# First head of each attention group turned by VectorE and through DRAM instead of by TensorE

## What is computed

```python
q = (x @ wq)            # 16 heads of 128
k, v = x @ wk, x @ wv   # 4 heads of 128, each shared by 4 query heads
# causal attention with a running softmax over chunks of 128 keys
x = layernorm(x + attention(q, k, v) @ wo)
logits = clip(xt @ gate_w.T, -50, 50)     # 8 experts, the two best per token
rw = softmax(top 2)
weighted = (softmax(expert_atom_weights) @ atoms) * sigmoid(importance)
# sparse expert rows: contrib[t, row] += x[t, col] * sum_k rw[t, k] * weighted[expert_k]
x = layernorm(x + xt @ W.T + contrib)
```

## Time and profile before

| | us |
|---|---|
| median of 3 runs | 1833.12 |
| profiled execution | 1836.27 |
| its span | 1834.5 |
| TensorE busy | 1774.3 (97%) |
| VectorE busy | 1238.0 (67%) |
| ScalarE busy | 823.1 (45%) |
| GpSimd busy | 799.0 (44%) |

### The profile page before, as it was taken

One profiled execution on the slowest core, in us unless ns is written; L12 is line 12 of the kernel. 1 busy time (PEld: TensorE's weight loads), 2 busy tenths in 40 slices (PEclk: granted clock), 3 DMA queues, 4 the chain that ended last, 5 costly groups with the idle time before them and its releaser, 6 DMA issues.

```text
span 1834.5 us, 33331 instructions
## 1 busy us (share of the span) xinstructions
PE 1774.3 (97%) x9290; PEld 1502.0 (82%) x9290; DVE 1238.0 (67%) x3881; ACT 823.1 (45%) x2058; POOL 799.0 (44%) x1093
## 2 busy tenths in 40 slices
PE   8999999999999999999999999999999999999982
PEld 7888888888888888888888888888888888778872
DVE  5566467776777577757775777677776777763355
ACT  4444344434444444544454444454444443434454
POOL 6775345544554333323332333233323334666564
PEclk9999999999999999999999999999999999999996
DMA  9665443335333455454444445454445338545788
GB/s 329 223 226 195 164 141 116 116 110 168 116 116 110 150 162 153 150 174 149 154 150 159 134 152 160 154 177 158 150 133 198 135 107 314 173 161 166 251 314 318
DMA packets 156287, 315.83 MB, mean 172 GB/s; under 512 B 23008, under 2 KB 66176, under 8 KB 145600
## 3 DMA queue, kind: packets, MB, share of 16 engines
q1 hardware_dynamic: 137808, 273.74, 44.2%
q0 software_dynamic: 18288, 39.80, 7.1%
HBM read 226.25 MB, written 87.23 MB: 171 GB/s over the span
## 4 chain that ended last, share of the span: by engine, by line
PE 85%; DVE 4%; issue 3%; POOL 2%; DMA 2%; ACT 1%; DVEq 0%; POOLq 0%; ACTq 0%; SPq 0%
PE psum L1541 23%; PE psum L1543 23%; PE psum L1542 23%; PE psum L1568 7%; PE psum L2298 2%; PE psum L2299 2%; PE psum L2300 2%; PE psum L372 1%; DMA token_rows<-x,ids_now 1%; ACT probs L1818 1%; PE psum L788 1%; DVE pT_lo L1942 1%; POOL expert_weights L1435 1%; POOL probs L1415 0%; DMA chosen_rows<-y_rows,slot_now 0%
## 5 line engine op out<-in xcount | busy, mean ns | idle before, releaser
L1415 POOL TENSOR_SCALAR probs<-probs,row_inv 128x128 f32<-128x128 f32 (+3 forms) x512 | 308.0, 625 | 435.1 <-DVE row_inv L1939 433.2
L1818 ACT ACTIVATE probs<-probs,neg_max 128x512 f32<-128x512 f32 (+3 forms) x512 | 282.4, 554 | 361.4 <-DVE neg_max L1931 359.4
L1541 PE MATMUL psum<-xT_hi,w_hi 128*128 128x512 f32 x640 | 252.5, 394 | 0.7 <-DVE qT_lo L1956 0.7
L1931 DVE CUSTOM_DVE_ANT_0 probs<-psum,causal 128x512 f32<-128x512 f32 (+3 forms) x512 | 223.4, 487 | 42.7 <-issue 20.4
L1543 PE MATMUL psum<-xT_hi,w_lo 128*128 128x512 f32 x640 | 250.2, 391 | 0.0
L1542 PE MATMUL psum<-xT_lo,w_hi 128*128 128x512 f32 x640 | 249.9, 390 | 0.0
L1942 DVE TENSOR_TENSOR pT_lo<-psum,pT_hi 128x512 fp32r<-128x512 f32 (+1 forms) x384 | 206.5, 593 | 19.7 <-ACT pT_hi L1828 19.5
L1828 ACT CAST pT_hi<-psum 128x512 fp32r<-128x512 f32 (+1 forms) x384 | 172.3, 526 | 65.2 <-PE psum L1568 65.2
L1541 PE MATMUL psum<-wo_hi,oT_hi 128*128 128x512 f32 x496 | 196.8, 397 | 0.0
L1543 PE MATMUL psum<-wo_hi,oT_lo 128*128 128x512 f32 x496 | 194.0, 391 | 0.0
L1542 PE MATMUL psum<-wo_lo,oT_hi 128*128 128x512 f32 x496 | 193.6, 390 | 0.0
(11 more groups left out here) (250 smaller groups left out, 3870.4 us busy)
## 6 DMA issues: line engine op xcount, KB each, us to landing
w_hi<-split_qk_weights SPq DMA_DIRECT2D x140, 256.0 KB, 2.7
w_lo<-split_qk_weights SPq DMA_DIRECT2D x140, 256.0 KB, 3.0
wo_hi<-split_out_weights SPq DMA_DIRECT2D x27, 1024.0 KB, 5.5
wo_lo<-split_out_weights SPq DMA_DIRECT2D x27, 1024.0 KB, 7.6
expert_weights_hi_lo<-split_expert_weights SPq DMA_DIRECT2D x8, 2048.0 KB, 10.0
x_in<-in_L_attn_x_dram SPq DMA_DIRECT2D x8, 1024.0 KB, 7.3
expert_weights<-fill SPq DMA_DIRECT2D x16, 512.0 KB, 4.4
piece_raw<-expert_weights SPq DMA_DIRECT2D x16, 512.0 KB, 5.9
```

The costliest lines, as they stand in the source:

```text
L1415: last = pool.tensor_scalar(p, p, row_inv[:, buf, i:i + 1], 1.0, ALU.mult, ALU.mult)
L1541: pe.matmul(dst, hi_s, hi_m, start=start, stop=False)
L1818: last = act.activation(probs[:, buf, a:a + w], probs[:, buf, a:a + w], ACT.Exp, bias=neg_max[:, buf, i:i + 1], scale=-1.0, accum_out=row_ ...
L1931: last = dve.tensor_tensor_reduce(probs[:, buf, a:a + w], psum[:, BANK_S + bank, col:col + w], causal[:, T - w:T], -1.0, -MASKED, ALU.add, ...
```

## The change

In batches 1 to 7, but not in the last iteration (`is_moved`), the first head of a group is not turned on TensorE. VectorE turns it in squares of 32 x 32 inside each 32 partitions (`turn_blocks`, 5 instructions, 1280 columns), SyncE stores the result to DRAM (`strips`) and reads it back with four transfers that put the squares at their partitions (`move`), and one copy of ScalarE and one subtraction of VectorE make the halves of all 1280 columns (`moved_pT`). Query 2 is projected right after scores(n + 1), and scores(n + 2) come ahead of the second filler. The fourth head is turned between query 0 and query 1 of the next iteration. In "group" iterations that are moved, the key is now projected ahead of values 0/1 and query 0 goes to the key's bank, as in "first" (`is_key_first`, `banks_as`). The buffers of the expert pieces become single ones to make room. On GpSimd `route_rstd` stands behind a `normalize` instead of ahead of it.

```diff
+SQUARE = 32
+SIDE = P // SQUARE
+MOVED_FROM = HKV
+MOVES = 16 * (1 + SIDE)
...
+        self.blocks = arena("probs_blocks", [P, SIDE, PACK // SIDE])
+        self.moved = moved("probs_moved", [P, SIDE, PACK // SIDE])
+        self.piece_raw = piece_raw("piece_raw", [P, PIECE * NE])
...
+def is_moved(kind, route):
+    return route and kind != "end"
+
+def is_key_first(kind, route):
+    return kind == "first" or is_moved(kind, route) and kind == "group"
+
+def lows_done(n, k, kind, route):
+    if is_moved(kind, route):
+        return 3 * (n + (0, 0, 1, 3)[k]) + 3
+    return 3 * (n + k) + 3
...
SyncE
+        def move(it, k, free):
+            wait_apart(sp, s_blocks, moved_number(it, k) + 1, s_passed)
+            sp.dma_start(strips[k], F.blocks[:].rearrange("p j f -> p (j f)")).then_inc(s_moved, 16)
+            wait_apart(sp, s_pt_lo, free, s_passed)
+            wait_apart(sp, s_moved, 32 + MOVES * moved_number(it, k), s_passed)
+            for j in range(SIDE):
+                src = strips[k, :, j * PACK // SIDE:(j + 1) * PACK // SIDE].rearrange("(i p) f -> p i f", p=SQUARE)
+                sp.dma_start(F.moved[j * SQUARE:(j + 1) * SQUARE], src).then_inc(s_moved, 16)
+
         def iteration(b, g, it, kind, route, job):
+            n = it * G
             after, second = (g + 1) % HKV, (g + 2) % HKV
+            if is_moved(kind, route):
+                move(it, 0, 3 * n)
             if route and kind == "first":
...
GpSimd
-            if route and kind != "first":
+            if route and kind == "end":
                 route_rstd(pool, R, it - TT)
             normalize(n + 1, 1)
+            if route and kind not in ("first", "end"):
+                route_rstd(pool, R, it - TT)
...
-            if route and kind == "first":
-                route_rstd(pool, R, it - TT)
             normalize(n + 2, 0)
+            if route and kind == "first":
+                route_rstd(pool, R, it - TT)
...
TensorE
+            pe.wait_ge(s_norm, n + k + 1)
+            pe.wait_ge(s_pt_lo, lows_done(n, k, kind, route))
...
             scores(n + 1, 1)
+            if moved:
+                pe.wait_ge(s_q_lo, n + 2)
+                query(2, it, BANK_A)
...
             filler(0 if kind == "first" else 1)
+            if moved:
+                scores(n + 2, 0)
+            else:
+                query(2, it, BANK_A)
...
-            transposes(n, 0)
+            if not moved:
+                transposes(n, 0, kind, route)
...
-            transposes(n + 1, 1)
-            scores(n + 2, 0)
+            transposes(n, 1, kind, route)
+            if not moved:
+                scores(n + 2, 0)
...
+            query(0, it + 1, bank_of_query(0, banks))
+            if moved:
+                transposes(n, 3, kind, route)
...
+            query(1, it + 1, bank_of_query(1, banks))
+            if not moved:
+                transposes(n, 3, kind, route)
             scores(n + 4, 0)
...
ScalarE
+        def moved_pT(n, it, k):
+            act.wait_ge(s_moved, 16 + MOVES * (moved_number(it, k) + 1))
+            act.wait_ge(s_o, n + 2 * k)
+            act.copy(pT_hi[:, 0].rearrange("p (b i c) -> p b i c", i=SIDE, c=SQUARE),
+                     F.moved[:].rearrange("p i (b c) -> p b i c", c=SQUARE)).then_inc(s_pt_hi, 3)
...
             exps(n + 1, 1)
+            if moved:
+                qT(n + 2, 0, BANK_A)
...
+            if moved:
+                exps(n + 2, 0)
+            else:
+                qT(n + 2, 0, BANK_A)
+                pT(it, 0, kind, route)
...
             if kind != "end":
                 qT(n + 3, 1, BANK_A)
...
+            if moved:
+                moved_pT(n, it, 0)
...
+                oT(n, 0, banks)
+                if not key_first:
                     kT(it + 1)
-                pT(n + 2, 0)
+                if not moved:
+                    pT(it, 2, kind, route)
             if kind != "end":
-                qT(n + 4, 0, bank_of_query(0, kind))
+                qT(n + 4, 0, bank_of_query(0, banks))
+            if moved:
+                pT(it, 2, kind, route)
+                pT(it, 3, kind, route)
             if kind != "end":
-                qT(n + 5, 1, bank_of_query(1, kind))
+                qT(n + 5, 1, bank_of_query(1, banks))
...
VectorE
             maxima(n + 1, 1)
+            if moved:
+                qT(n + 2, 0, BANK_A)
+                turn_blocks(n, it, 0)
+                inverse(n + 1, 1)
...
                 route_variance(dve, R, tt)
             if kind != "first":
                 add_rows(it - 1, 1, "group")
-            inverse(n + 1, 1)
+            if moved:
+                dve.wait_ge(s_blocks, moved_number(it, 0) + 1)
+                maxima(n + 2, 0)
+            else:
+                inverse(n + 1, 1)
+                qT(n + 2, 0, BANK_A)
+                pT(n, 0, moved)
...
+            if moved:
+                inverse(n + 2, 0)
...
+            pT(n, 1, moved)
...
+            if moved:
+                moved_pT(n, 0)
...
-                qT(n + 4, 0, bank_of_query(0, kind))
+                qT(n + 4, 0, bank_of_query(0, banks))
             if route:
                 route_chosen(dve, R, tt)
             if kind != "end":
-                qT(n + 5, 1, bank_of_query(1, kind))
-                pT(n + 3, 1)
+                if moved:
+                    pT(n, 2, moved)
+                    pT(n, 3, moved)
+                qT(n + 5, 1, bank_of_query(1, banks))
```

More of the change, by code:

```diff
@@ L1682, in values_first @@
                 pe.wait_ge(s_pt_lo, 3 * (n + 2) + 3)
-                values(n, 0, 0, kind)
+                values(n, 0, 0, banks)
                 if kind == "first":
@@ L1704, in turn_third @@
                 pe.wait_ge(s_o_lo, n + 1)
-                transposes(n + 2, 0)
+                transposes(n, 2, kind, route)
+            moved = is_moved(kind, route)
             scores(n + 1, 1)
+            if moved:
+                pe.wait_ge(s_q_lo, n + 2)
+                query(2, it, BANK_A)
             if kind != "first":
@@ L1734, in iteration @@
                 return
-            if kind == "first":
+            if kind == "first" and not moved:
                 filler(2)
@@ L1738, in iteration @@
             query(3, it, BANK_A)
-            if kind == "batch":
-                turn_x(b + 1, (0, 1))
+            if kind == "first" and moved:
+                filler(2)
+                scores(n + 3, 1)
+            if kind == "batch" and not moved:
+                turn_x(b + 1, (0, 1), route)
             filler(3)
             if kind == "batch":
-                turn_x(b + 1, (2, 3))
-            scores(n + 3, 1)
-            if kind == "first":
+                turn_x(b + 1, (0, 1) if moved else (2, 3), route)
+            if not (kind == "first" and moved):
+                scores(n + 3, 1)
+            if kind == "batch" and moved:
+                turn_x(b + 1, (2, 3), route)
+            key_first = is_key_first(kind, route)
+            banks = banks_as(kind, route)
+            if key_first:
                 pe.wait_ge(s_q_lo, n + 4)
@@ L1748, in iteration @@
             values_first()
-            if kind in ("group", "batch"):
+            if not key_first:
                 pe.wait_ge(s_q_lo, n + 4)
@@ L1878, in iteration @@
                 qT(n + 3, 1, BANK_A)
-            pT(n + 1, 1)
-            exps(n + 2, 0)
-            if kind == "first":
+            pT(it, 1, kind, route)
+            if not moved:
+                exps(n + 2, 0)
+            if kind == "first" and not moved:
                 v(b, 2)
@@ L1885, in iteration @@
             if kind == "first":
+                v(b, 2 if moved else 3)
+            if moved:
+                moved_pT(n, it, 0)
+            if kind == "first" and moved:
                 v(b, 3)
             if kind == "batch":
-                high_xT(act, F, psum, b + 1, range(C), BANKS_PT[:2])
+                high_xT(act, F, psum, b + 1, range(C // 2) if moved else range(C), BANKS_PT[:2])
             exps(n + 3, 1)
-            if kind == "first":
+            if kind == "batch" and moved:
+                high_xT(act, F, psum, b + 1, range(C // 2, C), BANKS_PT[:2])
+            key_first = is_key_first(kind, route)
+            banks = banks_as(kind, route)
+            if key_first:
                 kT(it + 1)
@@ L2037, in iteration @@
                 route_normalize(dve, R, tt)
-            inverse(n + 2, 0)
-            if early:
+            if not moved:
+                inverse(n + 2, 0)
+            if early and not moved:
                 route_logits(dve, R, tt, (2, 3), products)
@@ L2046, in iteration @@
                 qT(n + 3, 1, BANK_A)
+            if early and moved:
+                route_logits(dve, R, tt, (2,), products)
+            if moved:
+                moved_pT(n, 0)
             if late:
                 route_logits(dve, R, tt, (1, 2), products)
-            if kind == "batch":
+            if kind == "batch" and not moved:
```

(14 more changed lines are left out.)

177 lines of the change are left out of this document (94 added, 83 removed).

## The result

The kernel after took 2053.6 us (median of 4 runs, 2050.9 to 2058.5) beside 1833.2 us for the kernel before on the same chip: ratio 1.1206, 95% interval 1.1181 to 1.1231, slower by 221 us. The profiled execution took 2051.45 (span 2049.7), so 215.2 more than the 1836.27 of before. The forecast was 2028, in a range of 1955 to 2080.

The account below looks back on a forecast made before the run. TensorE, busy for 97% of the span, was taken to bound the kernel. -29.7 - 12 + 102.3 + 65.6 + 25.4 + 43 = +194.6 on 1836.3 gave 2031 us profiled, 2028 as a median, range 1955 to 2080.

Parts of the forecast that it names:

- Fourth turn: Between queries 0 and 1, TensorE waits 3.79 us for the third head's low halves in each of 27 iterations: +102.3 us.
- Opening: In 20 "group" and "batch" iterations, TensorE waits 1.64 us before scores(n + 2) and 1.64 before output row 2: +65.6 us.
- "First" iterations: In seven iterations, scores(n + 3) wait for the late route load, and in four scores(n + 2) wait 1.4 us: +25.4 us.
- Turns in squares: VectorE's block transposes of 1280 elements a partition, priced at 1.73 us, between bounds of 1.65 and 3.4.
- half-rate rival: VectorE's block transposes take 3.4 us instead of 1.73, lengthening the opening's second wait 20 times: 2061 us; chance 0.11.
- Removed: On TensorE, 27 turns of ten transposes go, -29.7 us, and the second turn's wait for low halves, -12 us.
- The clock: TensorE at half clock behind the new gaps, 1.7 us each: +37 us in the 27 iterations, +6 in "first".
- Eight in ten: Share of the 27 gaps of 3.8 us taken to have a half-clock stretch behind them: +37 us.
- The trip through DRAM: Storing the squares and reading them back is ready at about 19.8 us, before ScalarE asks at 20.1: no cost.
- late return: The four reads land some 4 us after ScalarE asks, so values(n) wait: 2082 us and more; chance 0.08.
- Cover holds: Third head's evacuation runs during query 0, so the fourth turn finds free banks: 1791 us with opening covered; chance 0.03.

Follow-up runs that it names:

- third-head-first kernel: Kernel after, with the third head's evacuation put ahead of query 0's halves on ScalarE and VectorE: 1911.5 us, ratio 1.0429.
- the order alone: Kernel before, with only the fourth turn between queries 0 and 1 and the third and fourth heads' evacuations behind query 0's halves: 1976.8 us, ratio 1.0777.
- the opening alone: Kernel after, outside "first": query 2 and the whole second filler ahead of scores(n + 2), add_rows(1) and inverse ahead of query 2's low half: 2048.6 us, ratio 1.1047.
- the filled gap: Kernel after, with 14 unused matmuls on TensorE between query 0 and the fourth turn: 2010.4 us, ratio 1.0966.
- four-orders kernel: three-orders kernel, plus VectorE's order changed so squares start sooner, and in "batch" ScalarE's copy behind the next x's high halves: 1831.8 us beside 1850.9, ratio 0.9903.
- three-orders kernel: Kernel after, with third head's evacuation ahead of query 0's halves, fillers and add_rows(1) earlier outside "first", route load ahead of move in "first": 1852.6 us, ratio 1.0105.

## Why the prediction was right, and where not

- **Fourth turn, +102.3.** Right in place, cause and number: 27 x 3.69 by the iteration shown makes 99.6; the idle time is 95.6. The 0.10 less is VectorE's low halves starting before the recorded end of `route_chosen`, where I had waited for that end. Shown by the third-head-first kernel (gap gone) and by the order alone in the kernel before (same gap without the squares).
- **Opening, +65.6.** 57.7 of idle time, at the two places named. The forecast had 1.64 for each; by TensorE's pace the iteration above has 1.68 and 1.52 (output row 2 at 738.09, where scores begun at 734.55 end 2.02 later). But "paid in full" holds for adding them, not for taking them away: the opening alone gave 21 to 29 us back, since the work behind the waits was itself late by half as much.
- **"First" iterations, +25.4.** 28.3 of idle time. The waits of scores(n + 3) are 23.5 of it (19.8 forecast) and hang on the route load, as its experiment shows by taking 20 of them away; scores(n + 2) wait 2.9 in all (5.6 forecast), and 1.9 are waits of the values for V's low halves, which I did not have.
- **Turns in squares, 1.73.** 1.67. The half-rate rival falls. The moved copy took 1.25 and its low half 1.49, both at the lower ends of their bounds.
- **Removed, -29.7 and -12.** TensorE has its 270 transposes fewer. The 12 us of the wait before a turn were too many. The 11.9 of the earlier trace rows is idle time of PEld, the weight loads, which run beside the matmuls; all of it lies in the changed iterations, but the matmuls themselves waited there only 4.3 us in seven places, or 7.7 by the starts of all turns. I had read a wait of the one for a wait of the other.
- **The clock, +43.** This term failed in size: 65.4. It is above even the 58 that I gave as its bound. "Eight in ten" was too few: 26 of the 27 gaps before the fourth turn have a stretch at the lower level at or behind their end, and six of the seven before scores(n + 3) in "first", where I took half. What I left out are stretches of 6.8 us in place of 3.4 (six of 35) and three behind the shorter gaps of the opening (1.88, 1.89 and 2.05 us), which the earlier trace rows with one gap of 1.89 without such a stretch had seemed to exclude. That makes 41 pieces of 3.41 us, 139.9 in all, where I had 25, less the 9.2 us that fall into idle time. The price of one was right: the filled gap gave back 1.6 us for each of 27, 44 in all, where I had 37.
- **What cancelled.** The clock's 22 us are as much as the 21 by which 2031 missed the profiled 2051. That the rest comes out is luck in part: the waits were 5.0 too high (181.3 forecast with the -12, and 176.3 more idle time measured), 7.8 stand in no term, and 4.6 went outside the iterations.
- **The trip through DRAM, 0.** Right for the kernel after alone, and for a reason that was not said: its cover was TensorE's own waits. The cover gone, it cost 25 us (20 in the traces). The rival "late return" named the transfer, but as an addition to the waits.
- **The other side.** "Cover holds" named ScalarE's order as the deciding point and 1791 as the time. The order did decide 142 us; but with it alone, or with all three, the time did not fall under 1833. It took the fourth set of orders, and what it reached is 1815 (0.9903 x 1833), not 1791.

What the idea is worth in this kernel is then: 27 turns of 1.10 us, 29.7, less 11.2 us more idle time in the iterations (17.4 in place of 6.2), and less 3.4 lost at the lower level, which is 15.1. The 27 iterations of the four-orders kernel are 19.1 us shorter than before; where the other 4 come from I did not trace.

## What to carry to other kernels

When a stage leaves the engine that sets the time, read for every step that moves with it which buffer it needs free, and where the instruction that frees it stands in the other engines' programs: here one evacuation behind the wrong neighbour cost 142 us, against 30 that the change could give. A latency that costs nothing in a stalled kernel is not free, and a wait taken away gives back only as much as the next one is early; so price transfers against the order that you mean to end with. And a wait of 3.5 us on TensorE cost some 5.1 us here (3.5 and the 1.6 of the filled gap), as the clock fell behind it.

## What the runs showed of the hardware

- Filling a gap of 3.5 us with matmuls whose result nobody reads, with the work behind it no sooner, made the kernel 44 us faster, 1.6 us for each of 27 gaps; 42 of the 44 are time at the lower level.
- The lower level came at or behind the end of 31 of 32 gaps of over 3 us in the kernel after and of four of seven between 1.75 and 3 us; in the filled kernel also of 3 of 20 of 1.4 to 1.75 us, in the kernel with three orders of none of its 57 gaps, which were all of under 2 us. In the four-orders kernel TensorE waits 1.81 to 1.82 us at the same place of six iterations, and a stretch at the lower level follows one of the six. What tells a gap of 1.9 us that is followed by it from one that isn't stayed open.
- VectorE turned 1280 f32 columns in 32 x 32 squares, five instructions with strided operands, in 1.67 us, the pace of the maxima over as many columns (1.65).
- From the last square to the copy that waited for the landing, the store, the four reads and 640 KB each way took 10.2 us in the three-orders kernel and 9.3 in the four-orders one; from the store's issue to that of the reads 5.0 and 3.1 of it.
